# A gated two-layer block in float32 on one core: Strassen's seven products instead of eight for the up and down layers

## What is computed

```python
q_emb = relu(q @ W3 + b3)                                   # 64 x 512, one gate per sequence
x1 = relu(((64 * v + v.sum(axis=1, keepdims=True)) * q_emb[:, None, :]) @ W2 + b2)
w_up = ((w_up_q - 7.5) * repeat(w_up_scale, 64)).T          # 512 x 2048, from 4 bit codes
x2 = relu(x1 @ w_up + b_up + x1 @ w_up_lora_a @ w_up_lora_b)
w_down = ((w_down_q - 7.5) * repeat(w_down_scale, 64)).T    # 2048 x 512
out = v + x2 @ w_down + b_down + x2 @ w_down_lora_a @ w_down_lora_b
```

## Time and profile before

| | |
|---|---|
| time, median of 3 runs | 833.25 us (833.24 to 834.16) |
| span of the profiled execution | 832.3 us |
| TensorE busy | 811.9 us, 98% |
| VectorE, ScalarE, GpSimd busy | 302.3, 239.4, 21.4 us |
| DMA traffic | 39.64 MB |

### The profile page before, as it was taken

One profiled execution on the slowest core, in us unless ns is written; L12 is line 12 of the kernel. 1 busy time (PEld: TensorE's weight loads), 2 busy tenths in 40 slices (PEclk: granted clock), 3 DMA queues, 4 the chain that ended last, 5 costly groups with the idle time before them and its releaser, 6 DMA issues.

```text
span 832.3 us, 9143 instructions
## 1 busy us (share of the span) xinstructions
PE 811.9 (98%) x3576; PEld 671.5 (81%) x3576; DVE 302.3 (36%) x450; ACT 239.4 (29%) x370; POOL 21.4 (3%) x16
## 2 busy tenths in 40 slices
PE   5799999999999999999999999999999999999998
PEld 4578888888888888888888888888888888888886
DVE  6888885322132331423223132332224222241111
ACT  3353442422232222322214222232223322132221
POOL 3411000000000000000000000000000000000000
PEclk9799999999999999999999999999999999999999
DMA  8910001500004000120004000040000300020001
GB/s 318 419 50 1 1 0 52 151 1 1 0 1 152 0 0 0 55 97 0 0 0 148 3 0 0 0 151 0 0 0 31 120 0 0 0 100 2 1 1 51
DMA packets 13697, 39.64 MB, mean 48 GB/s; under 512 B 1648, under 2 KB 1776, under 8 KB 11760
## 3 DMA queue, kind: packets, MB, share of 16 engines
q1 hardware_dynamic: 13392, 39.33, 13.5%
q10 hardware_dynamic: 288, 0.08, 0.0%
HBM read 31.01 MB, written 8.39 MB: 47 GB/s over the span
## 4 chain that ended last, share of the span: by engine, by line
PE 95%; DVE 4%; DMA 1%; issue 0%; ACT 0%; DVEq 0%; ACTq 0%
PE up_ps L488 15%; PE up_ps L489 15%; PE up_ps L490 15%; PE acc L488 14%; PE acc L489 14%; PE acc L490 14%; PE lora_ps L488 1%; PE scale_ps L488 1%; PE lora_ps L490 1%; PE scale_ps L490 1%; PE lora_ps L489 1%; PE scale_ps L489 1%; DMA biases<-in_biases 1%; DVE x_in L389 1%; DVE xm_lo L399 1%; DVE xm_hi L397 0%
## 5 line engine op out<-in xcount | busy, mean ns | idle before, releaser
L405 DVE TENSOR_TENSOR x_lo<-full,x_hi 128x512 fp32r<-128x512 f32 x160 | 110.5, 691 | 469.8 <-ACT x_hi L271 469.8
L269 ACT ACTIVATE full<-up_ps,biases 128x512 f32<-128x512 f32 x142 | 97.9, 689 | 508.9 <-PE up_ps L490 508.9
L488 PE MATMUL up_ps<-x_hi,w_up_hi 128*128 128x512 f32 x512 | 200.2, 391 | 0.7 <-DVE x_lo L405 0.7
L489 PE MATMUL up_ps<-x_lo,w_up_hi 128*128 128x512 f32 x512 | 200.1, 391 | 0.0
L490 PE MATMUL up_ps<-x_hi,w_up_lo 128*128 128x512 f32 x512 | 199.7, 390 | 0.0
L490 PE MATMUL acc<-x_hi,w_down_lo 128*128 128x512 f32 x512 | 199.2, 389 | 0.0
L489 PE MATMUL acc<-x_lo,w_down_hi 128*128 128x512 f32 x512 | 199.2, 389 | 0.0
L488 PE MATMUL acc<-x_hi,w_down_hi 128*128 128x512 f32 x512 | 199.2, 389 | 0.0
L488 PEld LDWEIGHTS up_ps<-x_hi,w_up_hi 128*128 128x128 f32 x512 | 96.4, 188 | 20.7 <-DVE x_lo L405 0.9
L490 PEld LDWEIGHTS up_ps<-x_hi,w_up_lo 128*128 128x128 f32 x512 | 96.5, 188 | 20.1
L489 PEld LDWEIGHTS up_ps<-x_lo,w_up_hi 128*128 128x128 f32 x512 | 96.6, 189 | 19.6
(11 more groups left out here) (68 smaller groups left out, 401.4 us busy)
## 6 DMA issues: line engine op xcount, KB each, us to landing
x_in<-in_x SPq DMA_DIRECT2D x32, 256.0 KB, 5.7
res<-in_x SPq DMA_DIRECT2D x8, 1024.0 KB, 6.8
out<-res SPq DMA_DIRECT2D x32, 256.0 KB, 2.7
codes_up<-in_q_up SPq DMA_DIRECT2D x3, 1024.0 KB, 18.7
codes_down<-in_q_down SPq DMA_DIRECT2D x3, 1024.0 KB, 21.1
raw_records<-in_records SPq DMA_DIRECT2D x3, 768.0 KB, 18.1
raw_w<-in_w SPq DMA_DIRECT2D x4, 256.0 KB, 7.9
raw_narrow<-in_narrow SPq DMA_DIRECT2D x1, 1024.0 KB, 11.4
```

Of the source, the lines that this page charges most:

```text
L269: act.activation(whole, source, ACT.Relu, bias=bias_col).then_inc(relu_done, 1)
L405: dve.tensor_tensor(lo, full[:, slot % FULL_SLOTS, :], hi.bitcast(F32), ALU.subtract).then_inc(act_split, 1)
L488: pe.matmul(dest, w_hi, a_hi, start=start, stop=False)
L489: pe.matmul(dest, w_hi, a_lo, start=False, stop=False)
```

## The change

The kernel is written anew around groups of 1024 tokens (`SBS` = 4 groups, two halves `j` of 512 tokens each).

The first group is computed as before, in three passes over plain weights, unit by unit. A unit is a pair of hidden tiles (`U`, 0 to 7) of up, or an output pair of down over four hidden tiles (`D`, four by two): 16 units, 48 matmuls each. For each unit the weight tile pairs are dequantized by DVE from codes and scales, the scales now arriving by DMA already repeated over partitions; PE makes the low-rank part with 4 matmuls of 256 columns (`low_rank`, L1101). In addition POOL makes the five sums and differences of weight blocks that Strassen's scheme needs (L688 to L691), ACT and DVE split them, and SP writes all seven, high and low, to a DRAM tensor `made_w` (1.835 MB a unit, 29.4 MB in all). So are the W2 weights (2.1 MB).

Groups 1 to 3 use Strassen's seven products. The 2 by 2 scheme is over (output half `a`, input half `i`) of the weights and (input half, token half) of the activations. A unit now costs 7 products of 2 tiles by 3 passes, 42 matmuls, where plain it costs 48. Its weights are streamed from DRAM into a ring of two units (`load_unit`, L280): 7 loads of 256 KB, each waiting for the same product of the unit two before. The code calls the products M1 to M7. PE's order in a slot is: M4 and M5 of unit n (`head`), M7 and M6 of unit n-1 (`tail`), M2, M3, M1 of unit n (`middle`). Products accumulate in four banks BA, BB, BP, BQ, of which each unit parity has four. Between them:

- ACT copies M4 out of BA (L451), and DVE writes M4 - M5 into BP before M1 adds to it (`share`, L822), and M3 waits for that;
- in up units, ACT copies BA after M2 (L458), DVE subtracts it from BP (`less_c21`, L828; M7 waits), then writes a sum into BQ (`begin_c22`, L835; M6 waits); in down units ACT copies BP to BQ (L481; M7 waits);
- ACT applies relu to the four banks of an up unit (L473), DVE makes four sums and differences (L878 to L884, five tiles of 512), ACT rounds seven tiles (L497 to L513), DVE makes seven low parts (L891); for x1 likewise once a group;
- DVE adds the four banks of a down unit to `res` (L846, L851), and POOL first corrects one quarter of `res` for the form of the scheme (L696, L698, two instructions of 1024 elements a group).

x is prepared with the gate multiply on ACT, 8 instructions of 64 columns a tile (L364), where it was one DVE instruction. W2 products stay plain, 96 matmuls a group. Summed over the program there are 3168 matmuls of 512 columns: 8 by 48 for W2 (384), 768 for the first group, 3 by 16 by 42 (2016) for the others.

```diff
-    PRODUCTS = []
-    for t in range(NH):
-        PRODUCTS += [("up", t)] + [("down", t - LAG)] * (t >= LAG)
...
+    MIDDLE = [("U", 0), ("U", 1), ("U", 2), ("D", 0, 0), ("D", 0, 1), ("U", 3), ("U", 4), ("D", 1, 0), ("D", 1, 1),
+              ("U", 5), ("U", 6), ("D", 2, 0), ("D", 2, 1), ("U", 7), ("W", 0), ("W", 1), ("D", 3, 0), ("D", 3, 1)]
...
+            def load_unit(s, n):
+                unit = slots(s)[n]
+                for o in range(7):
+                    occupant_done(sp, s, n, o)
+                    sp.dma_start(ring[n % 2][:, o].rearrange("p h v -> p (h v)").bitcast(F32),
+                                 made_w[uid(unit), W_PLACE[o]]).then_inc(w_loaded[n % 2][o], 16)
...
+            for s in range(1, SBS):
+                pool.wait_ge(res_loaded, 16 * s + 16)
+                pool.tensor_tensor(res[:, 2:4, 1, :], res[:, 2:4, 1, :], res[:, 0:2, 1, :], ALU.subtract).then_inc(res_fixed, 1)
+                pool.wait_ge(res_fixed, 2 * s - 1)
+                pool.tensor_tensor(res[:, 2:4, 1, :], res[:, 2:4, 1, :], res[:, 2:4, 0, :], ALU.add).then_inc(res_fixed, 1)
...
+            def head(s, n):
+                wait_bank(pe, BA, s, n)
+                product(s, n, M4, BA, True)
+                wait_bank(pe, BB, s, n)
+                product(s, n, M5, BB, True)
+            def middle(s, n):
+                ci = chain_no(s, slots(s)[n])
+                pe.wait_ge(s4_done, ci + 1)
+                product(s, n, M2, BA, False)
+                pe.wait_ge(e_done, ci + 1)
+                product(s, n, M3, BB, False)
+                product(s, n, M1, BP, False)
```

More of the change, by code:

```diff
@@ L48, in adaln_ffn @@
     ZERO_POINT = 7.5
[L49 to L65, removed]
@@ L80, in adaln_ffn @@
[L80 to L87, removed]
+    RING6 = 6
+    FIRST = [("U", 0), ("U", 1), ("D", 0, 0), ("D", 0, 1), ("U", 2), ("U", 3), ("D", 1, 0), ("D", 1, 1),
+             ("U", 4), ("U", 5), ("D", 2, 0), ("D", 2, 1), ("U", 6), ("U", 7), ("D", 3, 0), ("D", 3, 1)]
@@ L206, in adaln_ffn, with ring_round @@
+        def ring_round(s, n):
+            return sum(1 for s0 in range(1, s + 1) for n0, v in enumerate(slots(s0))
+                       if v[0] != "W" and n0 % 2 == n % 2 and (s0, n0) <= (s, n))
         block = ctx.enter_context(nc.Block())
@@ L261, in _ @@
+            s = SBS - 1
+            for dd in range(2):
+                for t, (a, j) in enumerate(((1, 0), (0, 1), (0, 0), (1, 1))):
+                    sp.wait_ge(res_done, 4 * down_no(s, 3, dd) + t + 1)
+                    sp.dma_start(out[s, :, dd + 2 * a, j * T:(j + 1) * T], res[:, dd + 2 * a, j, :]).then_inc(out_stored, 16)
+            sp.wait_ge(out_stored, 64 * (SBS - 1) + 128)
         @block.scalar
         def _(act):
-            def relu_tile(source, bias_col, n, slot, hi):
-                whole = full[:, slot % FULL_SLOTS, :]
-                act.wait_ge(product_ready, n + 1)
-                if not (isinstance(n, int) and n < FULL_SLOTS):
-                    act.wait_ge(act_split, n - FULL_SLOTS + 1)
-                act.activation(whole, source, ACT.Relu, bias=bias_col).then_inc(relu_done, 1)
-                act.wait_ge(relu_done, n + 1)
-                act.copy(hi, whole).then_inc(act_hi_done, 1)
@@ new lines, in product @@
+            def product(s, n, o, bank, start):
+                unit = slots(s)[n]
+                v = n % 2
+                pe.wait_ge(w_loaded[v][o], 16 * ring_round(s, n))
+                if unit == ("U", 0):
+                    pe.wait_ge(x1_split, 7 * (s - 1) + o + 1)
+                for q in range(2):
+                    if unit[0] == "U":
+                        high, low = (b[:, X_PLACE[o], q * T:(q + 1) * T] for b in (x1_hi, x1_lo))
+                    else:
+                        if unit[2] == 0:
+                            pe.wait_ge(x2_split[q], 5 * (up_no(s, 2 * unit[1] + q) // 2) + (1, 2, 2, 3, 4, 5, 5)[o])
+                        high, low = x2_hi[q][:, X_PLACE[o], :], x2_lo[q][:, X_PLACE[o], :]
+                    w = ring[v][:, o, :, q * P:(q + 1) * P]
+                    mm = three_passes(ps[4 * v + bank][:], w[:, 0], w[:, 1], high, low, start and q == 0, q == 1)
+                mm.then_inc(prod[o], 1)
```

1389 lines of the change are left out of this document (978 added, 411 removed).

## The result

| | before | after | forecast |
|---|---|---|---|
| time, median | 833.33 us (833.24 to 834.16, 4 runs) | 846.74 us (841.97 to 848.9, 4 runs) | 786.0 us |
| span of the profiled execution | 832.3 us | 845.7 us | 785.0 us |
| first plain unit starts | | 59.33 us | 54.6, and 1.8 of slow clock |
| first group from there | | 251.3 us | 204.9 us |
| groups 1 to 3 | | 531.7 us | 519.6 us |

The changed kernel is 1.5% slower: the ratio is 1.0149, with a 95% interval of 1.0119 to 1.0179. The prediction was wrong, in sign and by 61 us. The table's lower rows come from four starts in the timeline of TensorE in the kernel after (start us, length us, engine, line): first matmul of the first unit, last of the first group, first of group 1, last of all.

A forecast was written before the change was run, and what follows sets the result against it. It took the kernel as bound by its number of matmuls. Start 54.6 + 1.8, matmuls 696.4, low-rank 6.0, first group 3, later waits 19 and end 4.2 gave a 785.0 us span, 786 us measured; own range 775 to 800, overall 766 to 818.

The forecast's parts named there:

- 1.8 of slow clock: Behind TensorE's idle time at the start: 9 matmuls spaced at 0.43 us instead of 0.2267, 1.8 us.
- The first group: Units computed plainly after the start: VectorE, 9.1 us a unit, stays under TensorE's 11.34; 3 us of delays, bounds 0 and 35.
- The first rival: First group: VectorE and GpSimd exclude each other, so their times add, 13.8 us a unit for 11.34; 818 us, chance 0.12.
- The start: Before the first plain unit: W2 matmuls, idle time for low-rank tables, slow clock; together 56.4 us, bounds 48 and 64.
- Groups 1 to 3: Strassen groups: 2016 matmuls in 48 slots of 9.52 us, 192 for W2, and 19 us of waits, bounds 0 and about 60.
- GpSimd's corrections: Two instructions on `res` in slot 2 hold up VectorE and make `less_c21` late: 3 us a group, 9 in all.
- slots 4, 8 and 12: In groups 1 and 2, ScalarE's 16 gate multiplies there delay the copy to BQ: 3.0 us a group.
- The wait between groups: ScalarE rounds five x1 tiles in one row, making the copy behind them 1 us late, twice: 2 us.
- the last group's: The last group runs its final up units closer together: 2 us of waits.
- The spacing and the stream: Matmuls stay spaced at 0.2267 us; weight loads into the ring, 193 GB/s, are hidden at no cost.
- the end: After the last matmul, add and store: 4.2 us.
- The second rival: VectorE sets the pace of up units in groups 1 to 3, 33.6 us in place of 5: 815 us, chance 0.11.

The follow-up runs named there:

- the third version: ScalarE's gate multiply in the first group moved behind the third and fourth tiles' copies, against the kernel with loads before the store and x sums before `share`: 787.04 us.
- the first experiment: SyncE issues scales and codes of unit u+3 before the store of unit u's sums, against the changed kernel: 813.26 us, 0.975 of its time.
- the test in pieces: Each GpSimd correction of the residual issued as eight of 128 columns, against the kernel with the wide table's low parts on VectorE: 774.54 us, ratio 0.9295.

## Why the prediction was wrong

**The first group is the step that failed**, by 46.4 us of 60.7. The prediction asked whether VectorE is fast enough beside TensorE's 11.34 us a unit, added up 9.1 us of its work, and took 3 us. That sum was not what failed: with the loads ahead of the store, and ScalarE's multiply moved, the group takes 205.6 us against the forecast's 204.9. What it never asked is when VectorE's input lands. The loads are new DMAs of this change, they stand in SyncE's queue behind a store that waits for VectorE, and so VectorE's pace was tied to itself through a transfer. The rows needed were there: an issue of 256 KB landed after 5.7 us, and the 1.835 MB of sums and codes ahead of the scales take 5.2 more at the main queue's 350 GB/s, so 10.9 from the store's issue (10.2 measured). With VectorE's chain by the forecast's own prices, 1.25 + 1.38 + 1.6 = 4.2 us, a turn of 15.1 us could have been worked out, against 11.34. It was 15.23.

The order of the queue alone gives back 33.0 us of the group (251.3 to 218.3). The next 11.5 us (217.1 to 205.6) came from a second term that the prediction put at nothing: ScalarE's gate multiplies of the next x, 2.75 us a tile, ahead of the copies on the path. No run moved them alone in the changed kernel; that the loop's waits hid them there is argued from these two steps, not shown.

**The first rival** (port, 818 us) named the right stage and the wrong mechanism; filling in place of summing moved the span by 2.9 us, within the scatter of the changed kernel.

**The start** came 2.9 us later than the 56.4 forecast. The idle time for the low-rank tables was there, with the low-rank matmul at 35.2 us as forecast. GpSimd's three instructions took 9.6 us for the 9.7 forecast. What was left out is that VectorE stands still beside them and that ScalarE's four gate multiplies, 2.75 us each, hold the next W2 matmuls back by 3.6 us. The first W2 matmul came at 11.6 us for the 13 forecast, which hid a part of this.

**Groups 1 to 3** were forecast at 19 us of waits, and the gaps over 0.3 us sum to 20.7, nearly all in the places named: 2.2 us each in the fourth slot by GpSimd's corrections (3 forecast), and 1.4, 2.4 and 1.4 behind slots 4, 8 and 12 by ScalarE (5.2 a group, 3.0 forecast). The multiplies started 7.2 us into slot 8, as forecast, but the sixteen took 5.43 us for the 4.4 taken, and this 1.0 us is most of what each wait is over. The wait between groups (2) did not appear, and the last group's were 3.6 (2). Another 10.0 us are smaller excesses of the spacing, 6.1 of them at the slow clock's 0.43 us, for which the sum had no term; they make most of the 12.1 us that these groups were over.

**The spacing and the stream** were right: 0.2267 us (6.80/30, as from 310.62 us on, where six matmuls take 311.98 - 310.62 = 1.36 us), and no wait of TensorE on the ring's loads, at 200 GB/s over the span. So was the end, 3.4 us for 4.2. A slip that changed nothing: 37.7 MB in 174 us are 217 GB/s, not the 213 that the prediction gives as the most.

**The second rival** (VectorE's pace in groups 1 to 3) did not appear: with the waits cured, groups 1 to 3 take 505.6 us (262.56 to 768.20) for 500.6 of matmuls.

The forecast's 786 us is what the third version reaches (787.04). That does not make the prediction right: its terms were those of a kernel whose loads are always early, and here the queue's order decides that.

## What to carry to other kernels

When a change adds loads, write down for each what stands ahead of it in its issuing queue and what that waits for. If a store of an engine's results stands ahead of that same engine's next input, the turn (chain on the engine, plus issue to landing behind the store's bytes) is a bound on the pace like any engine's busy time; moving the loads ahead of the store cost four lines here and gave 33 us. And where GpSimd must work beside VectorE on a path that matters, issue its work in short pieces.

## What the runs showed of the hardware

- A short VectorE instruction can last as long as the GpSimd instruction beside it. At the start of the first experiment's kernel, an 8-column product of two SBUF inputs took 3.75 us instead of 0.17 and ended with GpSimd's 4.82 us instruction, while a reduction with one input ran at its usual 0.67 us:

```profile
30.34 4.82 POOL L679 TENSOR_TENSOR wide<-raw_tables,wide 64x2048 fp32r<-64x2048 f32 x1
...
30.74 0.67 DVE L706 TENSOR_REDUCE sums<-xt 128x8 f32<-128x512 f32 x1
31.44 3.75 DVE L715 TENSOR_TENSOR gated<-sums,gate 128x8 f32<-128x8 f32 x1
```

  The Trainium skill, page "SBUF — State Buffer", section "Who interferes with whom", calls this an exclusive lock for a whole instruction, and says that a reduction never contends. These rows agree, and so does the test in pieces. But what the lock costs the program is set by where it falls: at most 3.7 us over sixteen units in the first group, 11.4 us for six instructions in the later ones.
- A gap can cost more than its length, by the clock behind it. In groups 1 to 3 of the changed kernel five to eight matmuls behind four of the gaps are spaced at 0.43 us instead of 0.2267, which is the spacing that goes with a granted clock of 0.50, the lower of the clock's two levels, 1.2 GHz. Behind a gap of 2.27 us at 403 us the granted clock was 0.61 over the next 4 us; behind one of 2.17 us at 339 us it stayed at 1.00 (the third number from the right):

```profile
339.00:343.00 4.00, 3.53 (x14) 2.63 (x15) 3.97 (x6) 1.21 (x2) 0.00 (x0) 1.00 0.34 125
403.00:407.00 4.00, 3.94 (x11) 3.13 (x12) 1.39 (x2) 2.50 (x5) 0.00 (x0) 0.61 0.10 38
```

  So the length of a gap alone does not tell here. Removing 6.9 us of gaps in the later groups gave 11.4.
- The same 2048 columns by 64 rows took 4.82 us on GpSimd and 2.29 on VectorE (where the table was moved); eight ScalarE multiplies of 64 columns took 2.75 us, 0.34 each.
